# A convolution and routed expert block on one core: an order of its own for the three steps that take in no image, and the first weights centred in one product

## What is computed

```python
x = x + conv(ln_c(x))          # ln_c: over channels, for each pixel
    # conv: a, m = mean(x) @ w1.T + b1, max(x) @ w2.T + b2   (over the pixels of an image)
    #       taps = softmax of (m - a) over the 9 taps of a channel
    #       3x3 depthwise convolution with them, + bias, + x
t = tokens(x)                  # 32 * 1024 tokens of 128 values
    # gate = ln_t(t) @ Wg + bg ; the best two of 8 experts, softmax of their two logits
    # each: gelu(ln_t(t) @ W1[e] + b1[e]) @ W2[e] + b2[e], weighted
t = t + ffn(ln_t(t))
```

## Time and profile before

| | |
|---|---|
| median of three runs | 1591.4 us |
| the profiled execution | 1590.49 us, its span 1588.5 us |
| busy in the span | PE 1468.3 us, DVE 1372.5, ACT 1064.8, POOL 963.8 |

### The profile page before, as it was taken

How to read it: one execution, slowest core, us unless ns; L and a number is a source line. 1 busy time by engine, 2 the same in 40 slices (tenths; PEclk the granted TensorE clock), 3 DMA queues, 4 the chain that set the end, 5 groups by cost and what they waited for, 6 DMA issues and landing times.

```text
span 1588.5 us, 45185 instructions
## 1 busy us (share of the span) xinstructions
PE 1468.3 (92%) x12192; PEld 1128.6 (71%) x12193; DVE 1372.5 (86%) x2715; ACT 1064.8 (67%) x2402; POOL 963.8 (61%) x1057
## 2 busy tenths in 40 slices
PE   5899999999998768999999999999999999999765
PEld 2445455444545416999999999999999999999654
DVE  2568888888888866999999999999999999999654
ACT  4577777777777415777777777777777777777400
POOL 1004555446545675777777777777777777777500
PEclk7999999999999757999999999999999999999866
DMA  4202121212221172111111111111111111110199
GB/s 136 80 27 68 59 78 65 71 57 78 64 71 47 40 146 72 44 43 45 47 47 45 43 40 46 43 47 41 47 47 43 48 42 47 47 45 12 40 408 398
DMA packets 61998, 115.70 MB, mean 73 GB/s; under 512 B 15471, under 2 KB 39051, under 8 KB 61946
## 3 DMA queue, kind: packets, MB, share of 16 engines
q1 hardware_dynamic: 37210, 62.14, 12.8%
q0 software_dynamic: 18112, 34.27, 6.8%
q10 hardware_dynamic: 6624, 18.69, 3.2%
HBM read 60.08 MB, written 58.48 MB: 75 GB/s over the span
## 4 chain that ended last, share of the span: by engine, by line
POOL 33%; issue 27%; PE 23%; ACT 8%; DMA 5%; DVE 2%; POOLq 1%; SPq 1%; ACTq 0%; DVEq 0%
POOL token_out L505 17%; PE psV L820 12%; POOL yt L500 7%; POOL xn L493 7%; PE psV L771 4%; DMA ye<-token_out 4%; ACT spent L601 3%; PE psT L805 2%; PE psA L762 2%; PE psG L807 2%; POOL rows_by_pair L475 2%; ACT cv L589 1%; PE psV L999 1%; ACT sq L557 1%; DMA stage<-in_L_ffn_W_dram 1%
## 5 line engine op out<-in xcount | busy, mean ns | idle before, releaser
L1311 DVE TENSOR_TENSOR gl<-g,gh 128x512 f16<-128x512 f32 x620 | 519.9, 878 | 16.5 <-ACT gh L705 8.9
L505 POOL DMA_INDIRECT token_out<-yt,rt x310 | 391.1, 1262 | 185.0 <-POOL yt L500 132.7
L475 POOL DMA_INDIRECT rows_by_pair<-rows,idx x256 | 268.8, 1050 | 325.8 <-issue 202.4
L820 PE MATMUL psV<-lp,diag 128*128 128x512 f32 x576 | 275.3, 610 | 19.0 <-ACT cv L589 17.6
L705 ACT ACTIVATE gh<-g 128x512 f16<-128x512 f32 x465 | 274.5, 624 | 16.9
L698 ACT ACTIVATE g<-psT 128x512 f32<-128x512 f32 x310 | 181.9, 597 | 107.0 <-DVE gl L1311 77.9
L698 ACT ACTIVATE g<-psV 128x512 f32<-128x512 f32 x310 | 184.0, 597 | 90.5 <-PE psV L939 78.9
L960 PE MATMUL psR<-wall,gh 128*128 x1240 | 221.3, 273 | 0.6 <-DVE ya L1328 0.6
L960 PE MATMUL psG<-wall,gh 128*128 x1240 | 221.3, 273 | 0.0
L961 PE MATMUL psG<-wall,gl 128*128 x1240 | 213.0, 219 | 0.0
L961 PE MATMUL psR<-wall,gl 128*128 x1240 | 213.0, 219 | 0.0
(11 more groups left out here) (210 smaller groups left out, 2938.9 us busy)
## 6 DMA issues: line engine op xcount, KB each, us to landing
rt<-rows_by_pair SPq DMA_DIRECT2D x155, 133.0 KB
xb<-in_x_dram SPq DMA_DIRECT2D x32, 512.0 KB, 3.5
ye<-token_out SPq DMA_DIRECT2D x32, 512.0 KB, 7.9
out_dram<-oe ACTq DMA_DIRECT2D x32, 512.0 KB, 8.5
token_out<-yt,rt POOLq DMA_INDIRECT x310
rows_by_pair<-rows,idx POOLq DMA_INDIRECT x256, 2.4
stage<-in_L_ffn_W_dram SPq DMA_DIRECT2D x1, 2048.0 KB, 9.6
rows_by_pair<-pad_rows SPq DMA_DIRECT2D x15, 133.0 KB
```

The source lines that it names most:

```text
L475: gp.indirect_dma_start(rows_dram, bass.IndirectOffsetOnAxis(ap=idx[p][:, b:b + 1].bitcast(U32), axis=0), rows[p][:, b, :], None).then_inc ...
L505: gp.indirect_dma_start(y_dram, bass.IndirectOffsetOnAxis(ap=rt[r][:, b, ID:ID + 1].bitcast(U32), axis=0), yt[r][:, b, :], None, bounds_ch ...
L820: ins = te.matmul(psConv.rearrange("p (h w) -> p h w", w=WW), diag[k][:, m, :], lp[j][:, y:y + HH // 2, dx:dx + WW], start=(m == 0), stop= ...
L1311: v.tensor_tensor(gl[side][q][:, cols], g[side][:, cols], gh[side][q][:, cols], ALU.subtract).then_inc(lo_done, 1)
```

## The change

Steps 16 to 18 leave `run_steps` and are written out for PE, ACT and VectorE one after another. GpSimd and SP keep their order. The diff, without its context:

```diff
-            for s in range(LAST, NU + 3):
+            for s in range(LAST, NU):
                 step(Step(s // 2, s % 2))
...
# ACT
+            def high_w1(first, end):
+                for e in range(first, end):
+                    act.wait_ge(s_shift, e + 1)
+                    sc_.activation(wall_e[:, e, O_1H:O_1L], shift_bank[e], ACT.Copy, scale=WSCALE).then_inc(s_high, 1)
...
             run_steps(act, step)
+            s16, s17, s18 = LAST_STEPS
+            for k in range(2):
+                diagonals(s16, k)
+            token_std(s16, 0)
+            keep(s16, 0)
+            take(s16, 0, 0)
+            weights_of(s16)
+            take(s16, 0, 1)
+            token_std(s16, 1)
+            keep(s16, 1)
+            for h in range(2):
+                take(s16, 1, h)
+            weights_of(s17)
+            token_std(s17, 0)
+            keep(s17, 0)
+            high_w1(0, 4)
+            token_std(s17, 1)
+            keep(s17, 1)
+            weights_of(s18)
...
-            for e in range(E):
-                act.wait_ge(s_shifted, e + 1)
-                sc_.activation(wall_e[:, e, O_1H:O_1L], stage_1[:, e, :], ACT.Copy, scale=WSCALE).then_inc(s_high, 1)
+            high_w1(4, E)
...
# TensorE
+            def centre_w1(first, end):
+                if first == 0:
+                    pe.wait_ge(s_stage, 32)
+                    pe.wait_ge(s_b1, 1)
+                    pe.wait_ge(l_ready, NIMG)
+                    pe.wait_ge(cv_ready, 2 * NIMG)
+                else:
+                    pe.wait_ge(kept, NIMG)
+                    pe.wait_ge(lg_ready, NU)
+                    pe.wait_ge(rank_read, NU)
+                for e in range(first, end):
+                    te.matmul(shift_bank[e], centre_w[:, :], stage_1[:, e, :], start=True, stop=False)
+                    te.matmul(shift_bank[e], ident[0:E, e:e + 1].broadcast_to([E, P]), b1n[:, :], start=False, stop=True).then_inc(s_shift, 1)
             run_steps(pe, step)
-            pe.wait_ge(idx_ready, NU)
-            for e in range(E):
-                te.matmul(shift_bank[e], ones[:, :], stage_1[:, e, :], start=True, stop=False)
...
+            turn(s16, 0)
+            for m in range(len(taps_pe[0])):
+                conv(s16, 0, 0, m)
+            ranks(s16)
+            for m in range(len(taps_pe[0])):
+                conv(s16, 0, 1, m)
+            turn(s16, 1)
+            for h in range(2):
+                for m in range(N_PE):
+                    conv(s16, 1, h, m)
+            turn(s17, 0)
+            ranks(s17)
+            centre_w1(0, 4)
+            turn(s17, 1)
+            ranks(s18)
+            centre_w1(4, E)
...
# VectorE
-                v.tensor_scalar(b1n[:, :], b1r[:, :], -1.0, None, ALU.mult).then_inc(s_b1, 1)
+                v.tensor_scalar(b1n[:, :], b1r[:, :], 1.0 / D, None, ALU.mult).then_inc(s_b1, 1)
...
+            def low_w1(first, end):
+                for e in range(first, end):
+                    dve.wait_ge(s_high, 2 + e + 1)
+                    v.scalar_tensor_tensor(out=wall_e[:, e, O_1L:O_2], in0=shift_bank[e], scalar=WSCALE, in1=wall_e[:, e, O_1H:O_1L], op0=ALU.mult, op1=ALU.subtract).then_inc(s_low, 1)
             run_steps(dve, step)
+            first_choice(s16)
+            second_choice(s16)
+            window(s16, 3, 1, 0, N_DVE)
+            place(s16)
+            number(s16)
+            weigh(s16)
+            add_image(s16, 0)
+            window(s16, 2, 0, 0, N_DVE - 1)
+            shifts(s16)
+            first_choice(s17)
+            second_choice(s17)
+            add_image(s16, 1)
+            window(s17, 3, 1, 0, 1)
+            place(s17)
+            number(s17)
+            weigh(s17)
+            window(s17, 3, 1, 1, N_DVE)
+            low_w1(0, 4)
+            shifts(s17)
+            first_choice(s18)
+            second_choice(s18)
+            place(s18)
+            number(s18)
+            weigh(s18)
...
-            for e in range(E):
-                dve.wait_ge(s_shift, e + 1)
-                v.scalar_tensor_tensor(out=stage_1[:, e, :], in0=shift_bank[e], scalar=-1.0 / D, in1=stage_1[:, e, :], op0=ALU.mult, op1=ALU.add).then_inc(s_shifted, 1)
...
+            low_w1(4, E)
```

More of the change, by code:

```diff
@@ L176, in conv_moe_block @@
         s_high, s_low = sem("weights_high"), sem("weights_low")
-        s_shift, s_shifted = sem("shift_products"), sem("weights_shifted")
+        s_shift = sem("w1_centred")
         s_setup_pe = sem("setup_products")
@@ L312, in row_slot @@
                 return 2 if self.last(stage) else self.slot(stage)
+        LAST_STEPS = [Step(s // 2, s % 2) for s in range(NU, NU + 3)]
         def run_steps(eng, step):
@@ L617, in keep, with weights_of @@
                 sc_.activation(rows[p][:, blks, RSTD], rstd[st_.slot(3)][:, blks], ACT.Copy, scale=2.0).then_inc(kept, 1)
+            def weights_of(st_):
+                act.wait_ge(gap_ready, st_.count(4, 1, 1))
+                sc_.activation(e2[:, :, :], gaps[:, :, :], ACT.Exp).then_inc(e2_ready, 1)
+            def high_w1(first, end):
+                for e in range(first, end):
+                    act.wait_ge(s_shift, e + 1)
+                    sc_.activation(wall_e[:, e, O_1H:O_1L], shift_bank[e], ACT.Copy, scale=WSCALE).then_inc(s_high, 1)
             def step(st_):
@@ L627, in step @@
                     if k == 1 and st_.on(4):
-                        act.wait_ge(gap_ready, st_.count(4, 1, 1))
-                        sc_.activation(e2[:, :, :], gaps[:, :, :], ACT.Exp).then_inc(e2_ready, 1)
+                        weights_of(st_)
                     if st_.on(1):
@@ L888, in step @@
                         tap_logits(st_, quarter)
-            run_steps(pe, step)
[L893 to L898, removed]
-            pe.wait_ge(idx_ready, NU)
-            for e in range(E):
-                te.matmul(shift_bank[e], ones[:, :], stage_1[:, e, :], start=True, stop=False)
-                te.matmul(shift_bank[e], ident[0:E, e:e + 1].broadcast_to([E, P]), b1n[:, :], start=False, stop=True).then_inc(s_shift, 1)
+            def centre_w1(first, end):
[11 more added lines that the diff above has]
+                    te.matmul(shift_bank[e], ident[0:E, e:e + 1].broadcast_to([E, P]), b1n[:, :], start=False, stop=True).then_inc(s_shift, 1)
+            run_steps(pe, step)
+            s16, s17, s18 = LAST_STEPS
+            turn(s16, 0)
[14 more added lines that the diff above has]
+            centre_w1(4, E)
             pe.wait_ge(tab_in, 32)
@@ L1284, in _ @@
             v.tensor_copy(row_t[:, :, 0], trow[:, :]).then_inc(tab_ready, 1)
-            for e in range(E):
-                dve.wait_ge(s_shift, e + 1)
-                v.scalar_tensor_tensor(out=stage_1[:, e, :], in0=shift_bank[e], scalar=-1.0 / D, in1=stage_1[:, e, :], op0=ALU.mult, op1=ALU.add).then_inc(s_shifted, 1)
-            for e in range(E):
-                dve.wait_ge(s_high, 2 + e + 1)
-                v.scalar_tensor_tensor(out=wall_e[:, e, O_1L:O_2], in0=stage_1[:, e, :], scalar=WSCALE, in1=wall_e[:, e, O_1H:O_1L], op0=ALU.mult, op1=ALU.subtract).then_inc(s_low, 1)
+            low_w1(4, E)
             def low(j, r):
```

## The result

The changed kernel takes **1598.2 us**, the median of six runs (1596.9 to 1599.0), against 1591.5 for the kernel before in six runs of the same session (1590.0 to 1593.5): a ratio of 1.0041 with an interval of 1.0028 to 1.0054. It is slower by some 6.5 us. The prediction was 1597.4. The profiled execution after took 1598.5 with a span of 1596.5, which is 8.0 more than the one before.

The account below looks back on a forecast made before the run. GpSimd's scatters bound the kernel, pads and tables 5.1 us ahead of them. With pair 15's `idx` 11.3 later, pads end last and the first row load comes 6.0 later: 1590.5 + 6.0, with 0.9, 1597.4 us; range 1590.5 to 1600.0.

Parts of the forecast that it names:

- Pair 13 earlier: VectorE routes pair 13 at 532.0 instead of 538.26, so GpSimd starts its scatter at 532.9, 6.1 us earlier.
- the cover: ACT's `keep` waiting for pair 12's landed scatters is hidden on TensorE: cost nothing; if not, 1 us on all that follows.
- Four experts at the low clock: TensorE centres four experts ahead of the last turn at half clock: 16.0 us, 546.6 to 562.6, 6.0 behind the taps.
- the clock stays up: Rival, 14%: TensorE does the four experts at 2.4 GHz in 8 us; the first row load comes 2 to 4 us earlier.
- `idx` of pair 15: Last pair's index, after last turn, statistics, choices and ranking: at 581.0 instead of 569.35, taken as 11.3 us later.
- Off the path: VectorE's eight subtractions fall away; the second four experts take from about 580 to 596, halves to 602: all ahead of 610.
- Pads: Padding blocks and tile table, 29.6 us behind pair 15's `idx`, end at 610.3, 6.2 us past the scatters.
- the scatters' end: GpSimd idles from 575.8 to 582.6 ahead of pair 15 and ends near 603, giving back the 6.1 us.
- at best some 2 us less: Lower end for the pads' 29.6 us behind `idx`, if the last scatter ends ahead of them; first load then 4.2 later.

Follow-up runs that it names:

- the 128-row bias: Changed kernel with the bias row's product over all 128 partitions, 120 of them zeros, instead of 8: 1591.0 us, ratio 1.0000.
- all eight last: Changed kernel with all eight experts centred behind the ranking of pair 15, no early products: 1592.1 us, ratio 1.0005.
- The three kernels with the table early: Changed kernel with pair 15's taps ahead of pair 14's second choice (1590.8 us); that with 128-row bias products, experts spread (1589.8); that with three experts between turns (1592.0).
- the kernel with both edits: Changed kernel with pair 15's taps ahead of pair 14's second choice, 128-row bias products and early experts spread: 1589.8 us, ratio 0.9985.
- the one with three experts between the turns: Kernel with taps first, 128-row bias products and spread experts, but three instead of two experts between pair 15's turns: 1592.0 us, ratio 0.9987.
- the run with twice as many: Changed kernel with the four early experts' products issued twice, the second overwriting the first: 1610.2 us, measured once.

## Why the prediction was right

**The mechanism and the sum: right.** Six us were predicted for the first row load, 6.6 came in the profile, and 6.5 by the ratio (1.0041 of 1591.5).

- *Pair 13 earlier:* its first scatter was forecast at 532.9 with GpSimd behind pair 12; it came at 532.56. `keep` on ACT did wait for pair 12's rows, until 522.8, and the cover held: pair 14's ranking began at 544.85, forecast 545.3.
- *Four experts at the low clock:* forecast 546.6 to 562.6 at 0.50; measured 546.0 to 562.0 at 0.50. The rival that the clock stays up came true only with another mix of products, the 128-row bias, and from the middle of the set on. The reason that the prediction gave, the 32 us of the same mix in the earlier trace rows, was the right one to trust; what in the mix does it, the prediction did not ask.
- *`idx` of pair 15:* forecast 11.3 later, at 581.0; measured 11.25 later, at 580.6. Leaving out the early experts (e.g. all eight last) takes back 6 of it and the whole loss.
- *Off the path:* the second four experts ran from 579.4 to 595.4, forecast 580 to 596, and their halves on ACT and VectorE were over at 600.6, 10 us ahead of the last landing.
- *Pads:* forecast 29.6 us behind `idx`, so 610.3; measured 30.1, so 610.7. They decide, as forecast.

**Mis-sized: the scatters' end.** The step "GpSimd is idle from 575.8 to 582.6 and ends near 603, as before" was right for the issues (582.14, last 601.24) and wrong in what it left out: the earlier trace rows's 2.28 us from issue to landing was kept, when that scatter had been alone in the queues. Among the pads it took 8.4. So the pads decided by 1.1 us, not by 6.2. The time came out right because the later of the two was right, and with so small a margin that is in part luck. The lower end for the pads, "at best some 2 us less", was for a last scatter that ends ahead of them, which did not happen; with no scatter beside them at all they take 4.4 less (23.9 against 28.3).

**The rival that was wrong by this: the clock stays up.** It was priced at 2 to 4 us faster than before, on pads that end near 600 to 602 and scatters near 596. The run that is nearest to it, with the 128-row bias, issued its last scatter 6.5 us earlier than before, had its first row load only 1.0 earlier, and ended at a ratio of 1.0000. None of these orders got the gain that the change aimed at on GpSimd in full: the transfers behind it end at nearly the same time whichever comes first.

The Trainium skill (DMA: Bandwidth & Descriptors, "Queues, rings and completion order") says that each DMA engine takes packets in turn from the queues that have work. The landings of 2.3 to 2.5 us alone and 5 to 9 among the pads agree; how the turns are dealt out, no run here shows.

**Not foreseen: the clock at the start of phase B.** 1.3 of the 8.0 us of the profiled span. TensorE's last product before phase B ended at 595.4 in the changed kernel and at 601.6 before, and it waited 19.6 us instead of 6.8 for the first rows (TensorE's timeline of after, then of before):

```profile
614.98 0.69 PE L972 MATMUL psA<-ident,xn 128*128 128x128 f32 x2 [19.56 <-POOL xn L495]
```
```profile
608.35 0.69 PE L924 MATMUL psA<-ident,xn 128*128 128x128 f32 x2 [6.76 <-POOL xn L493]
```

That this wait is why the clock rose later is not borne out by the other traces: with all eight last TensorE waited 4.6 us there and then had half the clock for 4.7, with the 128-row bias it waited 27.2 and had it for 2.2. The cause stays open.

**What stays open.** The three kernels with the table early differ in the first row load by 1.4 us and in their ratios by less than their intervals; why the landing takes 4.9 us in one and 6.2 in another is not settled. Nor do the times follow that load to the microsecond: the kernel with both edits gains 0.15% (2.4 us) with a load 1.1 earlier than before, the one with three experts between the turns 0.13% (2.1 us) with a load 0.3 later, and the 128-row bias nothing with a load 1.0 earlier. From the first row load to the end the ten profiles take 983.4 to 986.0 us, so one profile of each can't tell where the rest lies; and the 1.4 us of the changed kernel behind that load are within this spread.

## What to carry to other kernels

An engine's idle time on the path is worth filling only up to the next resource: here the issues of the scatters could be brought 6 us forward, and the queues that they share with the padding took them back. Work put into a "free" stretch of TensorE has to be priced at the clock that the trace shows for that very mix of products, and against what waits behind it, here the last turn and through it the tables and pads. A duration from issue to landing holds only for the traffic that it was measured in.

## What the runs showed of the hardware

Products of 128 rows and of 8 rows in turn (fp32, 512 columns) ran for 16 us, and in the kernel before for 32 us, without a gap at a granted 0.50, 2.0 us each. Where such products had the full clock, in the run with twice as many, they lost it again at 551.0 while they ran. With the 8 rows filled up to 128 by zeros the clock rose in the middle of the set, and a product took 0.9, and 1.7 at the low clock before: rows of zeros made the four experts faster, 9.5 us instead of 16.0.

A scatter of 128 rows lands 2.3 to 2.5 us after its issue when nothing else moves, and 7.8 to 8.9 among 29 pads of 133 KB (changed kernel, all eight last, 128-row bias); the pads take 23.9 us alone and 28.3 beside sixteen scatters.
